# A preparation stage with two inverse roots placed in PSUM, an early root on ScalarE, and one step moved ahead of another on VectorE

## The chip, the cores and the metric

The kernel runs on one core of a Trainium2 chip. The metric is the device time of one execution in microseconds (us). Engines are named as in the profile: PE is TensorE's matmul (PEld its weight load), DVE is VectorE, ACT is ScalarE, POOL is GpSimd, SP is SyncE, which here only issues DMAs. "SPq" or "ACTq" is an engine's sequencer.

## The reference

Two layers over x of 16 batches, 512 tokens and 128 features, all fp32. Each layer adds an attention part and a feed-forward part to its input, both computed from the layer-normed input `xn`.

```python
# layer 0, attention part (16 heads of 8 features)
static_out = xn @ W.T
k = xn_by_head * rsqrt(mean(xn_by_head ** 2) + eps) * k_norm_w     # q = k
for each token:                                                    # gated delta rule
    S = lam * S
    S = S + beta * outer(k, v - k^T S)
    o = q^T S
out = layernorm(static_out + o) * o_norm_w + o_norm_b
# layer 0, feed-forward part: ternary weights 128 -> 512 -> 512 -> 512 -> 128
# layer 1: linear attention with a decay gamma ** position, and one linear map with a low-rank term
```

## The kernel before

The program has two blocks with a barrier between them. `prepare` computes, batch after batch, all that the token recurrence needs: the layer norm of x, the keys, the products of neighbouring keys, and a small triangular solve inside each group of four tokens. It stores the results to DRAM. `recur_and_second_layer` runs the recurrence, the feed-forward part and the second layer. The change lies wholly in `prepare`.

`prepare` is written by hand, engine by engine. Each engine runs its own list of steps in order, and semaphores tie the lists together. A loop counter k runs over the rounds, and one round works on four batches at once, each at another depth: batch k is normed, k-1 gets its keys, k-2 its products, k-3 its solve. DVE's round is:

```python
at(of(k), statistics)
at(of(k), aggregate)
if 0 <= k - 3 < NG - 1:
    lower(k - 3)
at(of(k - 1), square_sums)
at(of(k - 3), solve, 0)
at(of(k), scale)
at(of(k), offset)
at(of(k - 3), solve, 1)
at(of(k - 2), products)
at(of(k - 3), solve, 2)
at(of(k - 1), inverse_rms)
at(of(k - 1), keys)
```

- `scale` (L575) takes the reciprocal of the four standard deviations `std`; `offset` (L579) multiplies minus the mean (`mv`) by it to give `nm`. ACT's `norm` (L450) reads both and writes `xn`.
- `inverse_rms` (L590) takes 64 reciprocals; `keys` (L595) multiplies `xn` by them. PE's `keys` (L722) turns the result into `ps_k`.
- `solve` is `sweep` (L258 and L262), three times with 384, 256 and 128 elements. DVE's copy reads `ps_n` and keeps its product in `tmp_r`, which is a part of the PSUM bank `ps_t`. POOL does the same on SBUF tiles `tmp_p` and `pp`. POOL also scales the keys twice (L362, L370).
- `products` (L606) reads the keys in PSUM and in SBUF. PE's `couplings` (L737) reads the result, and ACT's `couplings` (L489) brings PE's result back for the next solve.
- PE's round is `static` (L729), `couplings` (L737), `keys` (L722), `normed` (L714), `factors` (L747), `weights` (L757). `weights` waits for ACT's `factors` (L496), which reads the bank that `factors` on PE has filled. PE's `factors` waits for DVE's `lower` (L623), which reads the bank that `weights` has filled. `lower` is there in ten of the rounds.

In round k = 1 DVE does two things once: `decays` (L643, L644), which waits for ACT's `exponentials` (L505, L506), and `added_row` (L652 to L657), which waits for the seven small DMAs of L324. POOL's `head_factors` (L415 to L427) waits for `decays`, and `products` waits for `head_factors`. PE starts with the transpose of W (L762) into `ps_t`, which waits for the DMA of W; ACT's `static_weights` (L510) copies it out. ACT loads a table of functions where a step needs another one than the step before.

## Time and profile before

| | us |
|---|---|
| median of 3 runs | 841.22 |
| lowest and highest of the 3 | 840.68, 842.06 |
| the profiled execution, its own time | 839.79 |
| its span in the profile | 838.1 |
| DVE busy in the span | 746.7 (89%) |
| PE busy in the span | 748.6 (89%) |
| POOL busy, ACT busy | 624.0 (74%), 590.5 (70%) |

The profile is of one execution. Its span runs from the first instruction of the program to the end of the last. The view of windows gives the busy time of each engine in a stretch of the span; the view of lines groups instructions by the line of the kernel and by shape; the timeline lists them in order of time, with the idle time before each in square brackets and what ended it; the view of waits sums that idle time by who waited for whom.

### The profile page before, as it was taken

Reading aid. Unit: us, or ns where it says so; the run is one execution under the profiler, and the core shown is the slowest. Engines: PE = TensorE matmul, PEld = TensorE weight load, DVE = VectorE, ACT = ScalarE, POOL = GpSimd, SP = SyncE. Lnnn points to the kernel's source line nnn. Section 1 sums busy time; section 2 is a strip of 40 time slices with the busy share of each in tenths; the row PEclk is TensorE's granted clock in tenths of the full one; section 3 lists DMA queues with packets and bytes.
Section 4 is the critical chain, followed back from the end, with each engine's and each line's share of the span. In section 5 each row is a group of like instructions: output and inputs, shape, how many; then the busy total and the mean of one; then the engine's idle time right before and its main releaser. Section 6 shows DMA issues by size and latency. Waiting matters only on the chain.

```text
span 838.1 us, 12725 instructions
## 1 busy us (share of the span) xinstructions
PE 748.6 (89%) x3427; PEld 533.7 (64%) x3427; DVE 746.7 (89%) x1391; ACT 590.5 (70%) x1349; POOL 624.0 (74%) x608
## 2 busy tenths in 40 slices
PE   3989797578999999999999999998679999999996
PEld 2544343246877877877887878885246666666664
DVE  5899999699999999999999999999868989899886
ACT  6887775577778878777797778777367666666631
POOL 3677879478697677777777767865579989899872
PEclk9899988689999999999999999999699999999999
DMA  5577554700600616115052143060133221312000
GB/s 150 178 256 255 203 195 155 174 22 14 139 24 15 138 38 137 38 38 113 24 108 68 38 89 74 0 174 23 34 110 101 64 89 56 97 51 63 14 27 26
DMA packets 136064, 75.68 MB, mean 90 GB/s; under 512 B 74826, under 2 KB 118860, under 8 KB 136012
## 3 DMA queue, kind: packets, MB, share of 16 engines
q1 hardware_dynamic: 134956, 74.58, 32.2%
q10 hardware_dynamic: 1056, 0.52, 0.2%
q8 instruction: 18, 0.29, 0.2%
q14 instruction: 34, 0.28, 0.1%
HBM read 39.86 MB, written 33.55 MB: 88 GB/s over the span
## 4 chain that ended last, share of the span: by engine, by line
DVE 51%; PE 25%; issue 3%; POOL 1%; DMA 0%; DVEq 0%; ACT 0%; SPq 0%; POOLq 0%
DVE r_rec L1138 12%; DVE r_pg L1132 11%; DVE r_kw L1141 11%; DVE r_gain L1146 11%; PE f_ps L1901 6%; PE f_ps L1902 6%; DVE r_rec L1151 6%; PE f_ps L1883 4%; PE r_rec L1936 2%; PE r_rec L1930 1%; PE r_rec L1920 1%; PE f_ps L1909 1%; DVE l_qs L1186 1%; PE r_rec L1918 1%; PE f_ps L1874 1%
## 5 line engine op out<-in xcount | busy, mean ns | idle before, releaser
L1263 POOL TENSOR_TENSOR f_hl<-f_h,f_hh 128x512 fp32r<-128x512 f32 x64 | 82.4, 1293 | 83.6 <-ACT f_hh L1516 83.5
L1380 POOL TENSOR_TENSOR l_kv<-l_qkv 128x1024 f32<-128x1024 f32 x64 | 125.0, 1952 | 23.7 <-PE f_ps L1902 21.0
L1776 PE MATMUL f_ps<-f_gh,w_hi 128*128 128x512 f32 x256 | 102.7, 401 | 7.6 <-POOL f_gl L1263 7.6
L1138 DVE TENSOR_REDUCE r_rec<-r_pg 128x64 f32<-128x576 f32 x128 | 97.4, 761 | 7.2
L1776 PE MATMUL f_ps<-f_hh,w_hi 128*128 128x512 f32 x256 | 101.3, 396 | 0.4 <-ACT f_b L1505 0.4
L1186 DVE TENSOR_TENSOR l_qs<-f_ps,l_qd 128x1024 f32<-128x1024 f32 x64 | 78.3, 1224 | 23.7 <-PE f_ps L1902 11.4
L1271 POOL TENSOR_TENSOR f_g<-f_a,f_b 128x512 f32<-128x512 f32 x64 | 82.0, 1294 | 16.2 <-ACT f_b L1505 16.2
L1146 DVE TENSOR_REDUCE r_gain<-r_kw 128x128 f32<-128x512 f32 x128 | 87.8, 686 | 4.4
L1263 POOL TENSOR_TENSOR f_gl<-f_g,f_gh 128x512 fp32r<-128x512 f32 x64 | 82.4, 1300 | 2.8 <-ACT f_gh L1511 2.8
L1193 DVE TENSOR_REDUCE l_o_in<-l_qs 128x128 f32<-128x1024 f32 x64 | 77.6, 1212 | 0.7
L1511 ACT ACTIVATE f_gh<-f_g 128x512 fp32r<-128x512 f32 x64 | 41.1, 642 | 52.2 <-POOL f_g L1271 51.7
L1778 PE MATMUL f_ps<-f_gl,w_hi 128*128 128x512 f32 x192 | 76.2, 397 | 0.0
L1778 PE MATMUL f_ps<-f_hl,w_hi 128*128 128x512 f32 x192 | 75.0, 391 | 0.0
L1776 PE MATMUL f_ps<-f_xh,w_hi 128*128 128x512 f32 x128 | 54.1, 423 | 22.9 <-ACT f_a L1501 14.8
L1901 PE MATMUL f_ps<-l_kv,tri 128*128 128x512 f32 x128 | 68.1, 614 | 6.7 <-DVE l_qs L1186 6.1
L1815 PE MATMUL f_ps<-w,f_e 128*128 128x128 f32 x512 | 69.6, 280 | 0.0
L1902 PE MATMUL f_ps<-l_kv,tri 128*128 128x512 f32 x128 | 66.2, 599 | 0.0
L1815 PEld LDWEIGHTS f_ps<-w,f_e 128*128 128x128 f32 x512 | 64.5, 198 | 0.0
L1515 ACT ACTIVATE f_h<-f_ps,t 128x512 f32<-128x512 f32 x64 | 44.7, 698 | 27.6 <-PE f_ps L1783 27.5
L1665 ACT ACTIVATE l_qkv<-f_ps 128x384 f32<-128x384 f32 x64 | 31.3, 489 | 46.4 <-PE f_ps L1883 44.9
L1776 PEld LDWEIGHTS f_ps<-f_gh,w_hi 128*128 128x128 f32 x256 | 49.4, 193 | 20.9 <-POOL f_gl L1263 8.6
L1883 PE MATMUL f_ps<-l_w_second,l_xnT 128*128 128x384 f32 x128 | 53.8, 503 | 2.5 <-ACT l_qkv L1665 0.9
(219 smaller groups left out, 2088.8 us busy)
## 6 DMA issues: line engine op xcount, KB each, us to landing
scratch_xnT<-p_xnT SPq DMA_DIRECT2D x16, 256.0 KB, 2.0
scratch_K<-p_kout SPq DMA_DIRECT2D x16, 256.0 KB, 2.3
scratch_fac<-p_fac SPq DMA_DIRECT2D x16, 256.0 KB, 2.0
scratch_R<-p_rr SPq DMA_DIRECT2D x16, 256.0 KB, 2.8
scratch_P<-p_pp SPq DMA_DIRECT2D x16, 256.0 KB, 2.4
first_x<-scratch_xnT SPq DMA_DIRECT2D x16, 256.0 KB, 2.8
first_xt<-in_L_attn_x_dram SPq DMA_DIRECT2D x16, 256.0 KB, 3.0
scratch_W<-r_w SPq DMA_DIRECT2D x16, 256.0 KB, 4.3
```

Source lines behind the costliest of these rows:

```text
L1132: dve.tensor_tensor(pg[q][:, at, :, :, 0:DH].rearrange("p (v g) i k -> p v g i k", g=G), by_head(state[q]), of_tokens(tok_p[u], t), ALU.mu ...
L1138: dve.tensor_reduce(w, pg[q][:, at, :, :, :], AX.X, ALU.add).then_inc(w_ok, 1)
L1141: dve.tensor_tensor(kw[:, :, :].rearrange("p (v g k) i -> p v g k i", v=DH, g=G), w.rearrange("p (v g) i -> p v g i", g=G).unsqueeze(3).to ...
L1146: dve.tensor_reduce(gain[:, :], kw[:, :, :], AX.X, ALU.add).then_inc(gain_ok, 1)
L1263: pool.tensor_tensor(lower, full, upper.bitcast(F32), ALU.subtract).then_inc(done, 1)
L1380: pool.tensor_tensor(dst, k, v, ALU.mult).then_inc(kv_ok, 1)
L1776: nc.tensor.matmul(bank, c.w_hi[:, weights[k], :], upper[k], start=k == 0, stop=False)
L1778: nc.tensor.matmul(bank, c.w_hi[:, weights[k], :], lower[k], start=False, stop=False)
L1815: ins = nc.tensor.matmul(y_at[:, tokens], e_f[:, k, tokens], c.w3[:, k, :], start=False, stop=t == NT - 1 and k == NB - 1)
L1883: nc.tensor.matmul(ps_q[:, 0:3, :].rearrange("p a b -> p (a b)"), xnT[m % XTS][:, t, :], w_second[:, 0:3 * P], start=True, stop=True).then ...
L1901: nc.tensor.matmul(ps_s[:, 0, :], c.tri[:, :], kv[s % 2][:, 0, :], start=True, stop=True)
L1902: nc.tensor.matmul(ps_s[:, 1, :], c.tri[:, :], kv[s % 2][:, 1, :], start=True, stop=True).then_inc(tri_mm, 1)
```

## The change

It makes five edits in `prepare`:

1. `rrms`, the 64 reciprocals that `keys` reads, is a part of the PSUM bank `ps_t` (columns 384 to 447) and no longer an SBUF tile. `tmp_r` uses columns 0 to 383 of that bank.
2. `scale` computes its four reciprocals twice, first into `rstd_ps` (columns 508 to 511 of `ps_t`), then into the SBUF tile `rstd`. `offset` reads the one in PSUM. ACT's `norm` reads the one in SBUF, as before.
3. ACT takes one square root of a constant before its first round, as soon as the constants are there.
4. In round 1, DVE's `added_row` stands ahead of `decays`.
5. The transpose of W goes to the bank `ps_s` in place of `ps_t`.

```diff
--- before.py
+++ after.py
@@ -154,10 +154,11 @@
         x_in = two("x", tile)
         stats = sb("stats", [P, NT, 6])
         mv = sb("mv", [P, NT, 2])
+        first_root = sb("first_root", [P, 1])
         std, rstd, nm = sb("std", [P, NT]), sb("rstd", [P, NT]), sb("nm", [P, NT])
         xn = two("xn", tile)
         sq = sb("sq", tile)
-        ssq, rms, rrms = sb("ssq", [P, NT * H]), sb("rms", [P, NT * H]), sb("rrms", [P, NT * H])
+        ssq, rms = sb("ssq", [P, NT * H]), sb("rms", [P, NT * H])
         keys_t = sb("keys", tile)
         xnT, kT = two("xnT", [P, L]), two("kT", [P, L])
         k2 = sb("k2", [P, L])
@@ -172,6 +173,8 @@
         ps_t = ctx.enter_context(nc.psum_tensor("p_ps_t", [P, L], F32))
         in_ps = ps_n[:, :, 0:NSEG * (BLK - 1) * BSEG].rearrange("p d (s n) -> p d s n", s=NSEG)
         tmp_r = ps_t[:, 0:(BLK - 1) * NSEG * BSEG].rearrange("p (d s b) -> p d s b", d=BLK - 1, s=NSEG)
+        rrms = ps_t[:, L - P:L - P + NT * H]
+        rstd_ps = ps_t[:, L - NT:L]
 
         x_ready = two_sems("x_ready")
         stat, aggregating, stat_ok, std_ok, rstd_ok, nm_ok = (sem("stat"), sem("aggregating"), sem("stat_ok"), sem("std_ok"),
@@ -507,7 +510,7 @@
 
                 def static_weights():
                     act.wait_ge(ws_tr, 1)
-                    act.activation(c.ws_t[:, :], ps_t[:, 0:P], ACT.Copy).then_inc(ws_ok, 1)
+                    act.activation(c.ws_t[:, :], ps_s[:, 0, :], ACT.Copy).then_inc(ws_ok, 1)
 
                 def lay_first_group():
 
@@ -530,6 +533,7 @@
                 act.sem_inc(coup_ok, 1)
                 act.sem_inc(fac_ok, 1)
                 act.wait_ge(const_done, 1)
+                act.activation(first_root[:, :], c.eps_ln[:, :], ACT.Sqrt)
                 for k in range(B + 3):
                     at(of(k), root)
                     at(of(k - 2), keys)
@@ -572,11 +576,12 @@
 
                 def scale(l):
                     dve.wait_ge(std_ok, l.count(1, 1))
+                    dve.reciprocal(rstd_ps, std[:, :])
                     dve.reciprocal(rstd[:, :], std[:, :]).then_inc(rstd_ok, 1)
 
                 def offset(l):
                     dve.wait_ge(rstd_ok, l.count(1, 1))
-                    dve.scalar_tensor_tensor(out=nm[:, :], in0=mv[:, :, 0], scalar=-1.0, in1=rstd[:, :],
+                    dve.scalar_tensor_tensor(out=nm[:, :], in0=mv[:, :, 0], scalar=-1.0, in1=rstd_ps,
                                              op0=ALU.mult, op1=ALU.mult).then_inc(nm_ok, 1)
 
                 def square_sums(m):
@@ -587,14 +592,14 @@
 
                 def inverse_rms(m):
                     dve.wait_ge(rms_ok, m.count(1, 2))
-                    dve.reciprocal(rrms[:, :], rms[:, :]).then_inc(rrms_ok, 1)
+                    dve.reciprocal(rrms, rms[:, :]).then_inc(rrms_ok, 1)
 
                 def keys(m):
                     dve.wait_ge(k_tr, m.count(1, 1))
                     dve.wait_ge(rrms_ok, m.count(1, 1))
                     dve.tensor_tensor(keys_t[:, :, :].rearrange("p t (h k) -> p (t h) k", h=H),
                                       xn[m.slot][:, :, :].rearrange("p t (h k) -> p (t h) k", h=H),
-                                      rrms[:, :].unsqueeze(2).to_broadcast([P, NT * H, DH]), ALU.mult).then_inc(keys_ok, 1)
+                                      rrms.unsqueeze(2).to_broadcast([P, NT * H, DH]), ALU.mult).then_inc(keys_ok, 1)
 
                 def products(n):
                     dve.wait_ge(n_mm, n.count(1, 1))
@@ -699,8 +704,8 @@
                     at(of(k - 1), inverse_rms)
                     at(of(k - 1), keys)
                     if k == 1:
+                        added_row()
                         decays()
-                        added_row()
                     largest(k)
                 powers()
                 whether_lower()
@@ -759,7 +764,7 @@
 
                 pe.wait_ge(const_done, 4)
                 pe.wait_ge(ws_in, 16)
-                nc.tensor.transpose(ps_t[:, 0:P], nat_ws[:, :], c.ident[:, :]).then_inc(ws_tr, 1)
+                nc.tensor.transpose(ps_s[:, 0, :], nat_ws[:, :], c.ident[:, :]).then_inc(ws_tr, 1)
                 for k in range(1, B + 3):
                     at(of(k - 2), static)
                     if k < B + 2:
```

Where it moves instructions. First DVE, around its one-time steps in round 1 (`p_work` are the decays, `one_rows`, `p_o_hi` and `ob_rows` the added row). Before:

```order
L590 RECIPROCAL p_rrms<-p_rms 128x64
L595 TENSOR_TENSOR p_keys<-p_xn,p_rrms 128x512
L643 TENSOR_SCALAR p_work<-p_work 128x2
L644 RECIPROCAL p_work<-p_work 128x2
L652 CAST one_rows<-p_ones 128x128
L653 CAST p_o_hi<-p_o_bias 64x128
L654 CAST ob_rows<-p_o_hi 32x512
L655 TENSOR_TENSOR ob_rows<-p_o_bias,p_o_hi 32x512
L657 CAST ob_rows<-p_o_bias 64x512
L563 BN_STATS p_stats<-p_x 128x6 x4
```

With the change, whose lines stand up to five further down:

```order
L595 RECIPROCAL p_ps_t<-p_rms 128x64
L600 TENSOR_TENSOR p_keys<-p_xn,p_ps_t 128x512
L657 CAST one_rows<-p_ones 128x128
L658 CAST p_o_hi<-p_o_bias 64x128
L659 CAST ob_rows<-p_o_hi 32x512
L660 TENSOR_TENSOR ob_rows<-p_o_bias,p_o_hi 32x512
L662 CAST ob_rows<-p_o_bias 64x512
L648 TENSOR_SCALAR p_work<-p_work 128x2
L649 RECIPROCAL p_work<-p_work 128x2
L567 BN_STATS p_stats<-p_x 128x6 x4
```

The five instructions of the added row stand ahead of the two of the decays, and the statistics of batch 2 still follow both. Then ACT at its start. Before:

```order
L526 DMA p_x<-in_L_attn_x_dram 128x4x128 x2
L444 ACT_TABLE_LOAD
L444 ACTIVATE p_std<-p_mv,eps_ln 128x4
L450 ACTIVATE p_xn<-p_x,p_nm,p_rstd 128x128 x4
L457 ACTIVATE p_sq<-p_xn 128x512
```

With the change:

```order
L529 DMA p_x<-in_L_attn_x_dram 128x4x128 x2
L536 ACT_TABLE_LOAD
L536 ACTIVATE p_first_root<-eps_ln 128x1
L447 ACTIVATE p_std<-p_mv,eps_ln 128x4
L453 ACTIVATE p_xn<-p_x,p_nm,p_rstd 128x128 x4
```

The load of the root's table stands at an instruction that waits only for POOL's constants, and the root of batch 0 follows without a load. Last, DVE in a middle round. Before:

```order
L262 TENSOR_TENSOR p_rr<-p_rr,p_ps_t 128x3x8x16
L575 RECIPROCAL p_rstd<-p_std 128x4
L579 SCALAR_TENSOR_TENSOR p_nm<-p_mv,p_rstd 128x4
L258 TENSOR_TENSOR p_ps_t<-p_ps_n,p_rr 128x256
L262 TENSOR_TENSOR p_rr<-p_rr,p_ps_t 128x2x8x16
```

With the change:

```order
L265 TENSOR_TENSOR p_rr<-p_rr,p_ps_t 128x3x8x16
L579 RECIPROCAL p_ps_t<-p_std 128x4
L580 RECIPROCAL p_rstd<-p_std 128x4
L584 SCALAR_TENSOR_TENSOR p_nm<-p_mv,p_ps_t 128x4
L261 TENSOR_TENSOR p_ps_t<-p_ps_n,p_rr 128x256
```

One reciprocal of four elements is added, and the instruction behind it has one input in SBUF and one in PSUM where it had two in SBUF.

## Rows read from the trace of the kernel before

**Rows 1.** Windows: stretch, us; busy us of PE, PEld, DVE, ACT, POOL; PE clock, DMA, GB/s.

```profile
27.00:110.00 83.00, 71.36 (x258) 36.52 (x257) 78.68 (x229) 65.91 (x158) 65.45 (x80) 0.92 0.70 232
110.00:155.00 45.00, 35.50 (x107) 16.22 (x105) 40.17 (x94) 29.46 (x67) 38.34 (x46) 0.89 0.45 161
```

**Rows 2.** Lines by shape, DVE, 0 to 160 us: busy us, mean ns, idle before.

```profile
L258 DVE TENSOR_TENSOR p_ps_t<-p_ps_n,p_rr 128x384 f32<-128x384 f32 x16 | 9.0, 560 | 4.3 <-ACT p_coup L489 4.3
L262 DVE TENSOR_TENSOR p_rr<-p_rr,p_ps_t 128x384 f32<-128x384 f32 x16 | 8.9, 554 | 0.5
...
L623 DVE TENSOR_TENSOR w_lo<-p_ps_f,w_hi 128x512 fp32r<-128x512 f32 x10 | 6.6, 658 | 0.0
```

**Rows 3.** One line each: durations in ns as least/median/most.

```profile
L579 DVE SCALAR_TENSOR_TENSOR p_nm<-p_mv,p_rstd x16: 161/600/995, 6.9 to 128.2; 128x4 f32<-128x4 f32 x16
...
L575 DVE RECIPROCAL p_rstd<-p_std x16: 168/170/177, 6.7 to 128.0; 128x4 f32<-128x4 f32 x16
...
L595 DVE TENSOR_TENSOR p_keys<-p_xn,p_rrms x16: 691/946/1575, 11.5 to 138.1; 128x512 f32<-128x512 f32 x16
```

**Rows 4.** Timeline, 69 to 70.4 us: start, us, engine, line, operation.

```profile
69.22 1.03 POOL L370 TENSOR_TENSOR p_kout<-p_kT,kfac 128x512 f32<-128x512 f32 x1
69.27 0.99 DVE L579 SCALAR_TENSOR_TENSOR p_nm<-p_mv,p_rstd 128x4 f32<-128x4 f32 x1
```

**Rows 5.** Timeline, the start of the program, 5 to 21 us.

```profile
5.07 1.28 ACT L444 ACT_TABLE_LOAD   x1 [5.07 <-DVE p_mv L570]
...
8.02 0.45 PE L762 MATMUL p_ps_t<-ident,p_nat_ws 128*128 128x128 f32 x1 [8.02 <-DMA p_nat_ws<-in_L_attn_W_dram]
...
9.14 0.58 SPq L324 DMA_DIRECT2D p_o_bias<-in_L_attn_o_norm_b_dram  x2
...
14.69 0.17 DVE L643 TENSOR_SCALAR p_work<-p_work 128x2 f32<-128x2 f32 x1 [2.51 <-ACT p_work L506]
...
14.97 0.21 DVE L652 CAST one_rows<-p_ones 128x128 fp32r<-128x128 f32 x1
...
16.98 0.87 DVE L563 BATCH_NORM_STATS2 p_stats<-p_x 128x6 f32<-128x128 f32 x4
...
18.40 0.30 ACT L444 ACTIVATE p_std<-p_mv,eps_ln 128x4 f32<-128x4 f32 x1 [2.45 <-DVE p_mv L570]
...
20.35 2.12 PE L729 MATMUL p_ps_s<-p_xnT,ws_t 128*128 128x512 f32 x2 [4.18 <-ACT p_xnT L466]
```

**Rows 6.** DMA issues, 3 to 11 us: KB each, median us from issue to landing.

```profile
p_x<-in_L_attn_x_dram SPq DMA_DIRECT2D x1, 256.0 KB, 3.0
```

**Rows 7.** Timeline of one middle round, PE, with DVE's last sweep and aggregation.

```profile
62.79 1.96 PE L729 MATMUL p_ps_s<-p_xnT,ws_t 128*128 128x512 f32 x2
...
63.79 0.29 DVE L262 TENSOR_TENSOR p_rr<-p_rr,p_ps_t 128x128 f32<-128x128 f32 x1
...
64.57 1.48 PE L737 MATMUL p_ps_n<-p_prod,head_ones 128*128 128x384 f32 x6
...
66.54 0.38 DVE L570 BATCH_NORM_AGGREGATE p_mv<-p_stats 128x2 f32<-128x6 f32 x4 [0.16 <-DVE p_stats L563]
```

**Rows 8.** Waits, 27 to 110 us: who waited for whom, us, times, longest.

```profile
PE p_ps_f L757 <- ACT p_fac L496: 10.3, 10, 1.8
...
PEld p_ps_f L747 <- issue: 2.1, 4, 0.8
```

**Rows 9.** Lines by shape, DVE, 27 to 110 us.

```profile
L595 DVE TENSOR_TENSOR p_keys<-p_xn,p_rrms 128x512 f32<-128x512 f32 x10 | 9.6, 956 | 1.0
...
L579 DVE SCALAR_TENSOR_TENSOR p_nm<-p_mv,p_rstd 128x4 f32<-128x4 f32 x10 | 6.9, 693 | 0.3
```

**Rows 10.** Waits, 110 to 132 us.

```profile
PE p_ps_n L737 <- DVE p_rr L262: 2.4, 3, 1.0
DVE p_ps_t L258 <- ACT p_coup L489: 0.7, 1, 0.7
```

**Rows 11.** Lines by shape, DVE, 110 to 132 us.

```profile
L579 DVE SCALAR_TENSOR_TENSOR p_nm<-p_mv,p_rstd 128x4 f32<-128x4 f32 x3 | 1.8, 598 | 0.1
```

## The prediction

> **What bounds the kernel now.** I began with the windows. The preparation ends at about 155 us, and the change touches nothing behind it. In its long middle, 27 to 110 us, DVE is busy 78.7 of 83 us and PE 71.4; from 110 to 155 us DVE is busy 40.2 of 45 us and PE 35.5 [rows 1]. So DVE is nearly full there, and PE is not far behind.
>
> Next, the lines by shape: does DVE's busy time consist of work? Two of its operations have durations that don't fit their size. `offset` (L579) works on four elements a partition and takes from 161 to 995 ns, while the reciprocal ahead of it on as many elements never takes over 177. `keys` (L595) takes from 691 to 1575 ns at one shape [rows 3]. The timeline shows what it is in one case: POOL starts a scaling of the keys at 69.22 and DVE `offset` at 69.27, and DVE's ends at 70.26, where POOL's ends [rows 4]. Both DVE operations have two inputs in SBUF, as POOL's has. The sweeps, which have one in PSUM, take 560 and 554 ns in the mean [rows 2] and show nothing like it. I read the excess as DVE standing at an SBUF interface that POOL holds.
>
> Third, the waits, for who takes over when DVE gets faster. In one middle round PE runs `static` from 62.79 to 64.75 and starts `couplings` right behind it at 64.57 (a matmul's end is modelled), while DVE's last sweep, for which `couplings` waits, was done at 64.08 [rows 7]. PE was the later one. Only ahead of `factors` (L747), which needs DVE's `lower`, does DVE hold it, and from 27 to 110 us that is 2.1 us in four waits [rows 8]. The 10.3 us in ten waits for ACT's factors [rows 8] are part of PE's own loop, since ACT waits for PE's matmul there. From 110 to 132 us it is the other way round: the weights are done, and PE waits for DVE's last sweep in each of three rounds, 2.4 us in all [rows 10].
>
> **The parts of the change.**
>
> *Inputs in PSUM, on DVE.* From 27 to 110 us there are ten rounds. `offset` falls from 693 ns to the 161 that it takes undisturbed: 10 x 0.53 = 5.3 us. `keys` falls from 956 to 691: 10 x 0.265 = 2.65 us [rows 3, 9]. The added reciprocal has no row at its place. A reciprocal of this size shows 170 ns [rows 3], which is the upper bound; four aggregations in a row take 0.38 us together [rows 7], so that one more small instruction behind another costs under 0.1, and I put the lower bound at 0.05. I take 0.1, because it too stands directly behind one without a wait between: -1.0 us. DVE is relieved by 6.9 us in this stretch.
>
> A PSUM operand could cost more than an SBUF one. The sweep that reads and writes PSUM takes 560 ns, the one that writes SBUF 554, and `lower` with one input in PSUM takes 658 for 512 elements [rows 2], under the 691 of `keys`. So I add nothing. The Trainium skill, in "VectorE: DVE Perf Modes" under "The TRN2 errata", gives VectorE 58 cycles of fixed cost from SBUF and 120 from PSUM at 0.96 GHz, which speaks against this change. By that rule, as an estimate, each of the 32 changed instructions would cost 65 ns more, 2.1 us of DVE in all, and the total below would be 0.2 smaller, since PE hides it in the middle. The rows do not bear it out.
>
> *What of it reaches the end.* In the middle PE takes over: of DVE's 6.9 us only the 2.1 that PE waited for `lower` come through. **2.1 us.** From 110 to 132 us DVE sets the pace in three rounds: `offset` saves 598 - 161 - 100 = 0.34 us each, 1.0 us [rows 3, 11]. `keys` stands ahead of DVE's wait for ACT's couplings, 0.7 us in one of these rounds [rows 10], so its 0.26 counts in one of the others, and perhaps in two. **1.3 us.** Behind 132 us no `offset` is left.
>
> *The root's table.* The load of 1.28 us at 5.07 waits for DVE's first statistics [rows 5]. Ahead of the first round it lies in the wait for x, and costs nothing: ACT has only issued two DMAs by then. The first batch is 1.28 us earlier, but PE waits for W's DMA until 8.02 [rows 5] ahead of its first transposes, so that some 0.3 us of it pass to what follows. The move of W's transpose to `ps_s` is one instruction for one, at the same time, and is costed at nothing; its bank is free until `static`.
>
> *The added row.* DVE idles 2.51 us ahead of the decays at 14.69, and the added row then takes from 14.97 to 16.98, 2.0 us [rows 5]. Put ahead, it fills the idle time. It adds a wait for the seven small DMAs, behind which decays, statistics of batch 2 and all of DVE are queued. The last of them are issued at 9.14 to 9.72 [rows 5]; the next DMA on the queue lands 3.0 us after its issue [rows 6], so I take 12.4 us. The row ends at 14.4, the decays are through at 14.8, and the statistics start there instead of at 16.98: 2.2 us earlier. They release ACT's root at 18.40, ACT's copies behind it release PE's `static` at 20.35, which PE had waited for during 4.2 us [rows 5], so all three engines move by this. POOL's head factors start no later than now. **2.2 us**, of which the table's 0.3 is a part; bounds 0.6 (should DMAs delay the row to 14) and 2.5.
>
> Sum: 2.1 + 1.3 + 2.2 = 5.6 us. The profiled execution takes 839.8 us by its own time, with 838.1 in its span and 1.7 around it, and would take 834.2. The median of the runs is 1.4 above it, so I predict **835.6 us**.
>
> **The rivals.**
>
> *PE does not bind (a chance of 0.12).* PE's loop holds modelled ends and granted clocks of 0.92 and 0.89 [rows 1]; were it to run at full clock more of the time because its own waits shrink, DVE's whole 6.9 us could come through in the middle: 2.2 + 6.9 + 1.3 = 10.4 us, 830.8 us. For it speaks that DVE is fuller than PE; against it, row by row, that PE's `couplings` started at PE's convenience in the middle.
>
> *The PSUM inputs don't help (0.15).* If DVE stood still for another reason, both operations keep their excess, and 16 reciprocals add 0.1 each, hidden in the middle, 0.3 behind it. Left are the head's 0.6 to 2.2 us: 839.3 to 840.9, of which half is within 0.2%. The even durations of the sweeps and of `lower`, which have one input in PSUM and run beside POOL [rows 2], speak against it. [...]
>
> *Partly swallowed (0.09).* The head's gain and the first rounds' are given back at a store or load that is late (DMA is 0.70 busy in the middle [rows 1]): a gain under 1.7 us, 840 us.
>
> *Slower (0.03).* The clock. PE has 0.92 and 0.89 of its clock in the preparation [rows 1], so some 8 of 83 and 5 of 45 us are lost to stretches at 1.2 GHz, half its full rate of 2.4. An earlier end moves all later stages against such stretches. For the whole to be slower by 1.7 us, over 7.3 us must be given back, that is 15 us more at 1.2 GHz than now. I price it at 843 us. Nothing in the rows asks for it.
>
> **How the numbers follow.** A measurement of this kernel can tell about 0.2%, 1.7 us, from no change. The forecast, 3.5 to 8 us gained, has 0.61. Faster: 0.61 + 0.12 + half of 0.15, 0.81 when rounded up; slower 0.03; the rest, 0.16, within 0.2%. The range leaves out the slower case, most of "PE does not bind" and the ends of the others: 832.3 to 839.5 us.
>
> **What would show it.** `offset` at 0.16 to 0.18 us in all 16 rounds and `keys` at 0.66 to 0.70, with little spread; the statistics of batch 2 near 14.8 and `static` of batch 1 near 18.2; from 27 to 110 us, DVE's busy share well below its 0.95, with waits ahead of the sweep for ACT's couplings, and PE without waits for `lower`; the preparation ending near 149.5 instead of 155. I am wrong in the middle if the rounds get shorter by over 0.4 us each, in the mechanism if `offset` still reaches 0.5 us, and in the head if the added row starts behind 13 us.

## The result, and the profile after

| | before | with the change |
|---|---|---|
| median, us | 841.64 | **835.51** |
| lowest and highest, us | 840.65, 844.67 | 830.63, 839.62 |
| executions | 8 | 8 |
| the profiled execution, its own time | 839.79 | 839.62 |
| its span | 838.1 | 837.9 |

The change makes the kernel faster, by a ratio of 0.9917 with a 95% interval of 0.9894 to 0.9940: 6 to 7 us. 835.6 was forecast. But the two profiled executions are almost equally long, since that of before is shorter than any of its eight comparison runs and that of the change is the longest of its eight. So the pair of traces alone would say that the change did nothing, and several things below rest on more than this pair.

The windows of the changed kernel, with the columns of [rows 1]:

```profile
27.00:110.00 83.00, 71.13 (x260) 37.57 (x260) 71.54 (x238) 65.33 (x158) 61.39 (x79) 0.92 0.71 231
110.00:155.00 45.00, 33.10 (x101) 15.42 (x100) 36.44 (x92) 27.92 (x62) 35.25 (x45) 0.83 0.48 171
```

DVE went from 78.7 busy us to 71.5 in the middle, while PE stays at 71.1. DVE has over 11 idle us there, and the clock of PE is no better than before. The three DVE operations that the edits touch, as in [rows 3] (ns, least/median/most):

```profile
L584 DVE SCALAR_TENSOR_TENSOR p_nm<-p_mv,p_ps_t x16: 157/159/160, 5.8 to 125.8; 128x4 f32<-128x4 f32 x16
...
L600 DVE TENSOR_TENSOR p_keys<-p_xn,p_ps_t x16: 687/687/689, 10.8 to 135.6; 128x512 f32<-128x512 f32 x16
...
L579 DVE RECIPROCAL p_ps_t<-p_std x16: 176/178/186, 5.5 to 125.6; 128x4 f32<-128x4 f32 x16
```

`offset` had taken up to 995 ns and `keys` up to 1575. Neither now varies by more than 3 ns. The start of the program, as in [rows 5]:

```profile
2.14 1.28 ACT L536 ACT_TABLE_LOAD   x1 [2.14 <-issue]
...
5.48 0.19 DVE L579 RECIPROCAL p_ps_t<-p_std 128x4 f32<-128x4 f32 x1 [0.36 <-ACT p_std L447]
5.57 0.15 DVE L580 RECIPROCAL p_rstd<-p_std 128x4 f32<-128x4 f32 x1
...
7.96 0.45 PE L767 MATMUL p_ps_s<-ident,p_nat_ws 128*128 128x128 f32 x1 [7.96 <-DMA p_nat_ws<-in_L_attn_W_dram]
...
12.47 0.23 DVE L657 CAST one_rows<-p_ones 128x128 fp32r<-128x128 f32 x1 [0.95 <-DMA p_o_bias<-in_L_attn_o_norm_b_dram]
...
14.43 0.17 DVE L648 TENSOR_SCALAR p_work<-p_work 128x2 f32<-128x2 f32 x1
...
14.71 0.85 DVE L567 BATCH_NORM_STATS2 p_stats<-p_x 128x6 f32<-128x128 f32 x4
...
18.07 2.12 PE L734 MATMUL p_ps_s<-p_xnT,ws_t 128*128 128x512 f32 x2 [3.38 <-ACT p_xnT L469]
```

The added row starts at 12.47 and the decays end behind it at 14.8. The statistics of batch 2 come at 14.71 in place of 16.98, and `static` of batch 1 at 18.07 in place of 20.35: 2.3 us earlier. The two reciprocals start 0.09 us apart.

Then the middle. PE's `factors` starts once a round, so the distance of its starts is the length of a round. The timeline of PE, from 47 us:

```profile
47.48 1.88 PE L752 MATMUL p_ps_f<-p_k,head_ones 128*128 128x512 f32 x2
...
58.95 1.87 PE L752 MATMUL p_ps_f<-p_k,head_ones 128*128 128x512 f32 x2
...
66.63 1.88 PE L752 MATMUL p_ps_f<-p_k,head_ones 128*128 128x512 f32 x2
...
74.32 1.88 PE L752 MATMUL p_ps_f<-p_k,head_ones 128*128 128x512 f32 x2
...
82.01 1.88 PE L752 MATMUL p_ps_f<-p_k,head_ones 128*128 128x512 f32 x2
```

One round takes 11.47 us and the next three 7.68, 7.69 and 7.69. Taken so, the first thirteen rounds of some executions are:

| | rounds, us | first ten |
|---|---|---|
| before | 7.63 8.08 8.36 8.61 8.06 8.65 7.75 9.40 8.41 8.53, 9.06 7.24 7.42 | 83.5 |
| change | 7.63 7.63 7.68 **11.47** 7.68 7.69 7.69 **11.25** 7.69 7.69, 6.75 **9.20** 6.75 | 84.1 |

The rounds of before vary. Those of the change are alike (7.63 to 7.69 us in the first ten, 6.75 behind them), except for three. Inside the first long one, the timeline of all engines:

```profile
50.44 0.60 ACT L482 ACTIVATE p_rr<-p_ps_s 128x512 f32<-128x512 f32 x1 [1.84 <-DMA scratch_R<-p_rr]
...
51.17 0.68 ACT L499 ACTIVATE p_fac<-p_ps_f,gate 128x512 f32<-128x512 f32 x1
...
51.99 1.08 PE L762 MATMUL p_ps_f<-ident,p_nath 128*128 128x128 f32 x4 [2.64 <-ACT p_fac L499]
...
54.68 2.74 PE L742 MATMUL p_ps_n<-p_prod,head_ones 128*128 128x384 f32 x6
...
57.52 0.93 ACT L492 ACTIVATE p_coup<-p_ps_n 128x384 f32<-128x384 f32 x3 [2.61 <-PE p_ps_n L742]
...
58.48 0.57 DVE L261 TENSOR_TENSOR p_ps_t<-p_ps_n,p_rr 128x384 f32<-128x384 f32 x1 [3.30 <-ACT p_coup L492]
```

Read it from the top. ACT's copy of `static` into `rr` (L482) waits 1.84 us for the store that still reads this buffer; `rr` has two. `factors` on ACT is queued behind it. PE's `weights` waits for that 2.64 us, where it waits 0.92 in an undisturbed round. And then the same six matmuls of `couplings` take 2.74 us, where they take 1.48 [rows 7]. The windows around it give the reason:

```profile
42.00:49.00 7.00, 6.41 (x26) 3.41 (x26) 6.64 (x24) 5.69 (x14) 5.15 (x7) 1.00 1.00 342
49.00:52.00 3.00, 0.36 (x2) 0.04 (x1) 2.83 (x9) 1.56 (x4) 2.88 (x4) 0.87 0.58 205
52.00:59.00 7.00, 7.00 (x25) 5.04 (x26) 3.54 (x12) 4.15 (x12) 2.88 (x5) 0.57 0.67 214
59.00:66.00 7.00, 6.08 (x23) 2.73 (x22) 6.60 (x24) 5.96 (x14) 5.82 (x8) 1.00 0.54 174
```

PE works 0.36 of 3 us from 49 to 52, and from 52 to 59 its granted clock is 0.57 in the mean, most of the time at 1.2 GHz in place of 2.4. PE is busy for all 7.00 us, and DVE and ACT wait for it. So a store for which ACT waits 1.8 us costs 11.47 - 7.69 = 3.8 us. The waits say how often this happened, from 27 to 110 us and then from 110 to 132:

```profile
PE p_ps_f L762 <- ACT p_fac L499: 12.5, 10, 2.6
...
DVE p_ps_t L261 <- ACT p_coup L492: 7.4, 4, 3.3
...
ACT p_rr L482 <- DMA scratch_R<-p_rr: 3.6, 2, 1.8
```

```profile
ACT p_rr L482 <- DMA scratch_R<-p_rr: 2.0, 1, 2.0
```

Two long rounds and then one: three waits, three long rounds.

An undisturbed round has PE's steps at fixed distances: `weights` 2.79 us behind `factors`, `couplings` 2.24 behind that, `keys` 1.31, `normed` 0.89, and the next `factors` 0.44. Ten such rounds make 76.8 us (two at 7.64, as the first two are, and eight at 7.69). What an execution takes more can be split: what `factors` comes later than 0.44 us behind `normed` is its wait for DVE's `lower`; the rest is everything else: late stores and the waits behind them, stretches at half clock, and `couplings` or `keys` that start later because DVE's results come later.

| first ten rounds, us | sum | above 76.8 | wait for `lower` | rest |
|---|---|---|---|---|
| before | 83.5 | 6.7 | 2.0 | 4.7 |
| change | 84.1 | 7.3 | 0.0 | 7.3 |

PE no longer waits for `lower`, the 2.1 us of [rows 8] are gone, and the rest is larger in this execution. (That row names "issue" and not `lower`; but in each of those rounds `lower` ends 0.10 us before `factors` starts.) Whether the change makes it larger is a question for the experiments.

### The profile page after: what moved, and what is told of

It reads as the page before. It is cut to its first block, busy times and chain, and to the rows that moved or that the text cites. A ratio compares the mean times of both kernels' runs of the same rounds, so it can differ in the third digit from the quotient of the medians.

```text
span 837.9 us, 12741 instructions
## 1 busy us (share of the span) xinstructions
PE 747.6 (89%) x3427; PEld 534.2 (64%) x3427; DVE 740.3 (88%) x1407; ACT 591.0 (71%) x1350; POOL 619.2 (74%) x608
## 4 chain that ended last, share of the span: by engine, by line
DVE 51%; PE 25%; issue 3%; POOL 1%; DMA 1%; ACT 0%; DVEq 0%; SPq 0%; POOLq 0%
DVE r_rec L1143 12%; DVE r_pg L1137 11%; DVE r_kw L1146 11%; DVE r_gain L1151 11%; PE f_ps L1906 6%; PE f_ps L1907 6%; DVE r_rec L1156 5%; PE f_ps L1888 4%; PE r_rec L1941 2%; PE r_rec L1935 1%; PE r_rec L1925 1%; PE f_ps L1914 1%; DVE l_qs L1191 1%; PE r_rec L1923 1%; PE f_ps L1879 1%
## 5 line engine op out<-in xcount | busy, mean ns | idle before, releaser
L1268 POOL TENSOR_TENSOR f_hl<-f_h,f_hh 128x512 fp32r<-128x512 f32 x64 | 82.6, 1296 | 83.1 <-ACT f_hh L1521 83.0
L1781 PE MATMUL f_ps<-f_xh,w_hi 128*128 128x512 f32 x128 | 54.1, 423 | 22.4 <-ACT f_a L1506 14.8
```

Source lines behind the costliest of these rows:

```text
L1268: pool.tensor_tensor(lower, full, upper.bitcast(F32), ALU.subtract).then_inc(done, 1)
L1781: nc.tensor.matmul(bank, c.w_hi[:, weights[k], :], upper[k], start=k == 0, stop=False)
```

## The experiments

Twelve runs follow, two of them repeats of the kernels themselves, each beside the kernel before on the same chip. "Preparation ends" is the start of the second block's first load in the profiled execution.

| | median, us (lowest to highest, runs) | before | ratio, 95% | preparation ends |
|---|---|---|---|---|
| before, first trace | | | | 158.97 |
| change | 835.51 (830.63 to 839.62, 8) | 841.64 | 0.9917 (0.9894 to 0.9940) | 156.78 |
| e1, change again | 834.80 (833.17 to 838.95, 6) | 841.71 | 0.9918 (0.9900 to 0.9936) | 155.70 |
| e2, head only | 839.31 (836.82 to 840.86, 11) | 841.71 | 0.9962 (0.9948 to 0.9976) | 159.09 |
| e3, PSUM only | 838.67 (838.08 to 838.90, 5) | 841.71 | 0.9961 (0.9946 to 0.9976) | 157.44 |
| e4, twins in SBUF | 839.56 (837.59 to 843.25, 12) | 841.71 | 0.9978 (0.9965 to 0.9992) | 157.49 |
| e5, third `rr` | **829.60** (827.59 to 831.49, 5) | 842.33 | **0.9840** (0.9819 to 0.9861) | 149.03 |
| e6, less on DVE | 837.66 (835.64 to 838.36, 4) | 842.33 | 0.9934 (0.9910 to 0.9959) | 155.39 |
| e7, two roots | 836.29 (834.69 to 837.73, 4) | 842.33 | 0.9927 (0.9902 to 0.9953) | 155.11 |
| e8, row only | 839.54 (837.63 to 842.48, 10) | 842.33 | 0.9967 (0.9953 to 0.9980) | 158.40 |
| e9, before again | 842.51 (839.81 to 844.27, 10) | 841.47 | 1.0003 (0.9984 to 1.0023) | 161.79 |
| e10, before, third `rr` | 838.30 (836.21 to 841.51, 10) | 841.47 | 0.9964 (0.9943 to 0.9985) | 156.77 |
| e11, third `rr` and `pp` | 830.11 (826.74 to 832.92, 6) | 841.47 | 0.9854 (0.9826 to 0.9883) | 148.50 |
| e12, offset only | 837.39 (834.89 to 838.77, 10) | 841.47 | 0.9944 (0.9927 to 0.9961) | 153.70 |

### Is the trace of the change an odd one? (e1)

The changed kernel without an edit, for a second profile.

> The changed kernel as it is, for a second profile and more times. Theory: the time of an execution hangs on how many rounds of the preparation are long (over 9 us where the others take 7.7), because a store of rr lands late, ACT's copy waits, PE stands idle and its clock falls to 1.2 GHz. Then this profile has another number of such rounds than the three of the first profile (839.6 us), each worth some 2 to 4 us, and the times spread over 830 to 840 us with a median near 835.5. Rival: the spread arises in the second block; then the preparation ends at the same 156.8 us in both profiles, and the difference of the spans lies behind it.

The second profile has the same three long rounds, of 11.74, 10.65 and 8.91 us, and 7.64 to 7.69 in the others of the first ten. ACT waits for the stores of `rr` 5.7 us in all (6.4 in the first profile). So the long rounds belong to this kernel and not to one execution. This profiled execution was again the longest of its kernel, 838.95 us; its preparation is 1.1 us shorter than the first's, and the second block 0.4 us longer. Why the profiled executions of the change are long was not found.

### The parts alone (e2, e3, e8)

e2 has the root's table and the added row, with the inputs in SBUF as before (edits 3 and 4). e3 has the inputs in PSUM and W's transpose (edits 1, 2 and 5), and e8 the added row alone (edit 4). The edits, in part:

```diff
 # e2, against the change; W's transpose goes to ps_t again
-        rrms = ps_t[:, L - P:L - P + NT * H]
-        rstd_ps = ps_t[:, L - NT:L]
-                    dve.reciprocal(rstd_ps, std[:, :])
 # e3, against the change
-                act.activation(first_root[:, :], c.eps_ln[:, :], ACT.Sqrt)
-                        added_row()
                         decays()
+                        added_row()
 # e8, against before
+                        added_row()
                         decays()
-                        added_row()
```

> Only the early root and the added row ahead of the decays (edits 3 and 4). Theory: PE's static of batch 1 starts at 18.1 us instead of 20.35, and the preparation ends 2.2 us earlier: a median of 839.3 (before 841.5). Offset keeps its 160 to 995 ns and keys its 690 to 1575. Rival (the head's gain is given back in the middle by the late DMAs): static at 18.1, but 841 us.

> Only the inputs in PSUM (edits 1, 2 and 5). Theory: offset at 0.16 us and keys at 0.69 in all rounds, undisturbed rounds of 7.7 us instead of 8.1 to 8.6, and a gain of 3.4 us, 838 us, with a spread of several us. Rival (PE alone binds and the DVE relief is worth nothing): under 1 us gained, 840.7 or more.

> Only the added row ahead of the decays (edit 4), with the table loaded where it was. Prediction's terms: the row starts when the small DMAs are in, near 12.4 us or when keys of batch 0 is done at 12.2, the decays wait for ACT's exponentials until 14.7, so the statistics of batch 2 start at 15.0 instead of 16.98, and PE's static of batch 1 at 18.4: 1.9 of the head's 2.2 to 2.3 us, a median of 839.7. Rival (the early table is what counts): static at 19 us or later.

The head is worth 2.4 us (841.71 to 839.31), and the PSUM inputs 3.0 (to 838.67). Together that is 5.4, and the whole change made 6.1 and 6.9 in its two comparisons, so that the parts add up within what the intervals leave. In e2 `offset` still takes up to 1.08 us and `keys` up to 1.18; in e3 they take 0.16 and 0.69 in all 16 rounds, and `static` of batch 1 starts at 20.37, as before. Of the head, the row alone is worth 2.8 us in its own comparison. Its timeline:

```profile
12.16 0.23 DVE L652 CAST one_rows<-p_ones 128x128 fp32r<-128x128 f32 x1
...
14.57 0.17 DVE L643 TENSOR_SCALAR p_work<-p_work 128x2 f32<-128x2 f32 x1 [0.47 <-ACT p_work L506]
...
14.85 0.85 DVE L563 BATCH_NORM_STATS2 p_stats<-p_x 128x6 f32<-128x128 f32 x4
...
18.20 1.11 PE L729 MATMUL p_ps_s<-p_xnT,ws_t 128*128 128x512 f32 x1 [2.15 <-ACT p_xnT L466]
```

`static` starts at 18.20 without the early table, against 18.07 and 18.11 with it. So the table is worth 0.1 us there and not the 0.3 of the prediction. The reason stands in the second row: the row ends before 14.1, and what remains is a wait of 0.47 us for ACT's exponentials. The table moves only that wait. The row itself starts at 12.16 here, right behind `keys`, but waits for its DMAs until 12.47 and 12.53 in the two traces with the table. With a row as early as here the table would be worth up to 0.45 us, as an estimate (14.57 less the 14.12 at which the row would let the decays start).

### Is it the port? (e4, e12)

e4 keeps every instruction of the change, also the second reciprocal, but puts both results into SBUF. e12 puts only that of `keys` back.

```diff
 # e4
-        rrms = ps_t[:, L - P:L - P + NT * H]
-        rstd_ps = ps_t[:, L - NT:L]
+        rrms = sb("rrms", [P, NT * H])[:, :]
+        rstd_ps = sb("rstd_two", [P, NT])[:, :]
 # e12
-        rrms = ps_t[:, L - P:L - P + NT * H]
+        rrms = sb("rrms", [P, NT * H])[:, :]
```

> The whole change, but rrms and the second copy of the four reciprocals lie in SBUF tiles, so that offset and keys have two inputs in SBUF again. Theory (POOL holds an interface that the second SBUF input needs): offset again takes up to 1 us and keys up to 1.6, rounds are 8.1 to 8.6 us, and only the head's 2.2 us are left, less 0.1 us a round for the added reciprocal: 839.5 to 840.5. Rival (what helps is the second instruction or the separate tile, not the place): offset at 0.16 to 0.2, 835.5.

> The change without edit 1: rrms back in SBUF, so that keys has two inputs in SBUF, while offset keeps one in PSUM. Theory: keys at 0.69 to 1.6 us again, offset at 0.16; undisturbed rounds of 7.7 to 8.1 us, about 1 us of the gain lost: 836 to 837 us. Rival (keys alone matters, since it stands ahead of ACT's couplings): 838.5 us or more.

Two lines in e4:

```profile
L584 DVE SCALAR_TENSOR_TENSOR p_nm<-p_mv,p_rstd_two x16: 161/670/935, 5.6 to 126.8; 128x4 f32<-128x4 f32 x16
...
L600 DVE TENSOR_TENSOR p_keys<-p_xn,p_rrms x16: 692/930/1433, 10.8 to 136.6; 128x512 f32<-128x512 f32 x16
```

and in e12:

```profile
L584 DVE SCALAR_TENSOR_TENSOR p_nm<-p_mv,p_ps_t x16: 157/159/160, 5.8 to 122.9; 128x4 f32<-128x4 f32 x16
...
L600 DVE TENSOR_TENSOR p_keys<-p_xn,p_rrms x16: 691/692/1592, 11.0 to 132.7; 128x512 f32<-128x512 f32 x16
```

The place of one operand decides, operation by operation, and nothing else in the change does. That it is POOL that DVE stands for, no run without POOL's work shows; the traces show it by coincidence in time. In the trace of before, each of the 13 `offset`s that take 320 ns or more ends 0.02 us behind the end of an instruction of POOL, and the three that take under 170 meet none. In the changed kernel 12 of the 16 run wholly inside an instruction of POOL and take no longer for it:

```profile
67.65 1.00 POOL L265 TENSOR_TENSOR p_pp<-p_pp,p_tmp_p 128x384 f32<-128x384 f32 x1
...
67.88 0.16 DVE L584 SCALAR_TENSOR_TENSOR p_nm<-p_mv,p_ps_t 128x4 f32<-128x4 f32 x1
```

e4 ends where e2 and e8 do (839.56 against 839.31 and 839.54), which leaves the whole gain of the middle to that place. In e12 `keys` is undisturbed in most rounds though it has two inputs in SBUF: with `offset` at a constant length, DVE mostly starts `keys` in a gap of POOL or just ahead of its next instruction. In the second case it is POOL that takes longer: its scaling that starts at 61.64, 0.02 us behind `keys`, takes 1.58 us where 1.04 is usual. Even so, e12 at 0.9944 is behind the whole change at 0.9917. The Trainium skill, in "SBUF — State Buffer" under "Who interferes with whom", gives VectorE and GpSimd one shared pair of ports with an exclusive lock; e4 and e12 agree with it, up to 0.9 us for one `keys` (1592 against 691 ns).

### Who binds the short rounds? (e6, e7)

e6 takes work away from DVE: from batch 3 on it leaves out the statistics and their aggregation for all but the first 128 of 512 tokens. e7 adds work: a second reciprocal of 64 elements whose result nobody reads.

```diff
 # e6
-                    for t in range(NT):
+                    for t in range(NT if l.off < 3 else 1):
 # e7, ahead of the reciprocal into rrms
+                    dve.reciprocal(idle_root[m.slot][:, :], rms[:, :])
```

> The whole change, with the statistics of batches 3 to 15 taken over the first 128 of their 512 tokens alone, the other three quarters being those of earlier batches: some 0.8 us less on DVE in each round. It tells whether DVE or PE sets the undisturbed rounds of 7.7 us. Theory of the prediction (PE's own loop binds): these rounds stay at 7.6 to 7.7 us, and the time within 1.5 us of 835. Rival (DVE is still full and binds too, both at 7.69): rounds of 6.9 to 7.3 us and 828 to 831 us.

> The whole change, with the 64 reciprocals of each batch computed once more into a tile that nothing reads: 0.48 to 0.55 us more on DVE in each round, where nothing but DVE does it. If DVE had room behind PE, undisturbed rounds stay at 7.7 us. If DVE is as full as PE there, as its 0.16 us of idle time in such a round says, they grow to 8.2 us, and the time rises by 3 to 5 us to 838 to 840 us.

The middle of e6, as a window and as two successive first sweeps of DVE:

```profile
27.00:110.00 83.00, 71.79 (x261) 37.17 (x261) 65.13 (x180) 65.39 (x159) 62.27 (x80) 0.92 0.71 231
```

```profile
66.04 0.56 DVE L261 TENSOR_TENSOR p_ps_t<-p_ps_n,p_rr 128x384 f32<-128x384 f32 x1 [0.70 <-ACT p_coup L492]
...
73.82 0.56 DVE L261 TENSOR_TENSOR p_ps_t<-p_ps_n,p_rr 128x384 f32<-128x384 f32 x1 [0.80 <-ACT p_coup L492]
```

DVE has 6.4 us less to do than in the change, and six of the ten rounds take 7.63 to 7.69 us as before, none less. In the two shown DVE waits 0.7 and 0.8 us. (The other four are 11.42, 7.78, 8.77 and 9.74 us; ACT waits for stores of `rr` around them.) So DVE does not set a round of 7.69. What is left is PE's loop, with the 0.92 us in which it waits for ACT's factors, and the change has brought DVE just below it.

e7 shows the other side. The extra reciprocal costs DVE some 0.5 us a round, and four of the ten rounds are 7.96 to 8.09 us, where PE again waits for `lower` (1.4 us in all). I had expected 838 to 840 us; it took 836.29, a ratio of 0.9927 against the change's 0.9917. The expectation was missed because the long rounds are shorter, 9.84 and 10.27 us in place of 11.47 and 11.25, at a granted clock of 0.83 in place of 0.70. In the first of them the store is less late (ACT waits 1.12 us, 1.84 in the change), in the second it is not (1.75 against 1.79), and why that one is shorter too was not found. One more round takes 8.53 us at a clock of 0.80, without a late store. Its first ten rounds sum to 83.8 us, those of the change to 84.1. So what DVE takes or gives in the other rounds was offset in the long ones, and the time hardly moved.

### The late stores (e5, e10, e11)

e5 is the change with three tiles for `rr` and a semaphore for each; to free one, the load of gamma is counted together with two others, in e11 also the last weight with `lower`. e10 is the kernel before with the same edit. e11 is e5 with three tiles for `pp` too. The edits, in part:

```diff
 # e5 and e10; e11 has the same for pp and st_p
-        rr, pp = two("rr", [P, L]), two("pp", [P, L])
+        rr, pp = [sb(f"rr{u}", [P, L]) for u in range(3)], two("pp", [P, L])
+        st_r = [sem(f"st_r{u}") for u in range(3)]
...
-                    reuse(act, st_r[m.slot], both(m))
+                    reuse(act, st_r[m.off % 3], 32 * (m.off // 3))
```

> The whole change, and a third tile for rr, the solved values that are stored to DRAM, so that ACT's copy of batch n waits for the store of batch n-3 and no longer of n-2 (one semaphore less elsewhere: gamma's DMA is counted with first_in). Theory (late stores of rr make ACT wait, then PE idles and loses half its clock): no wait of ACT's copy for scratch_R, no round over 8.5 us, twelve rounds of 7.7 us and less, the preparation ends some 6 to 9 us earlier in the profile, and the median falls from 835 to 829 to 832. Rival (the long rounds come from the clock or from DMA load as such): long rounds stay at 9 us or more, within 1 us of 835.

> The kernel before with the third tile for rr alone. Theory (DVE sets its rounds of 8.1 to 8.6 us, the late stores add little there): rounds of 8.0 to 8.3 us without long ones, and 2 to 4 us gained, 838 to 840 us; the third tile is worth 5 to 6 us only where DVE has been relieved. Rival (the two add up and have nothing to do with each other): 6 us gained, 836 us or less.

> The change with the third tile for rr and one more for pp, which POOL's scaling waits for (POOL waited 7.9 us in all for stores of pp in the run with the third rr; PE's w3 signal is counted with lo_done to free a semaphore). Theory (POOL is not on the loop that sets the rounds, but ACT's couplings wait for its solve once or twice): 0 to 2 us better than 829.6 us. Rival (POOL's lateness passes to SP's stores and from there to x): 3 us or more better.

The windows of e5, and its PE at the place of the long round (its lines stand two further down than those of the change):

```profile
27.00:110.00 83.00, 73.91 (x282) 37.03 (x283) 77.94 (x261) 71.98 (x174) 67.83 (x87) 1.00 0.76 249
```

```profile
47.75 1.88 PE L754 MATMUL p_ps_f<-p_k,head_ones 128*128 128x512 f32 x2
50.54 0.63 PE L764 MATMUL p_ps_f<-ident,p_nath 128*128 128x128 f32 x4 [0.92 <-ACT p_fac L501]
...
52.79 1.48 PE L744 MATMUL p_ps_n<-p_prod,head_ones 128*128 128x384 f32 x6
...
55.43 1.88 PE L754 MATMUL p_ps_f<-p_k,head_ones 128*128 128x512 f32 x2
```

The round takes 7.68 us. The first ten are all between 7.63 and 7.69, 76.8 us in all, against 84.1 for the change: nothing is left above the undisturbed rounds. PE has its full clock through the whole middle, `weights` waits 0.92 us and never more, and ACT has no wait for a store of `rr` in the whole preparation. It ends at 149.03, 7.8 us before that of the change. **829.6 us, 1.6% under the kernel before**: this version beats both kernels.

e10 separates the two: the third tile alone is worth 3.2 us on the kernel before (841.47 to 838.30). On the changed kernel it is worth 5.8 to 6.6 (the 12.7 of e5 less the 6.1 or 6.9 of the change). The split of the rounds says why. In e10 `offset` still reaches 0.99 us and `keys` 1.24; the rest is down to 2.3 us, but PE waits 3.9 us for `lower`. With no late stores the rounds fall back on DVE, unless DVE too has been relieved.

The 2.3 us are DVE's too, though ACT waits for no store of `rr` in e10. The windows from 27 to 110 us and of its round from 58.59, and the waits of PE's weight loads for DVE's products from 27 to 110 us in e10 and in e5:

```profile
27.00:110.00 83.00, 71.16 (x261) 34.71 (x260) 78.66 (x230) 67.32 (x161) 66.60 (x81) 0.98 0.71 234
58.59:67.12 8.53, 7.61 (x27) 4.15 (x27) 8.13 (x24) 6.49 (x17) 6.80 (x9) 0.80 0.80 253
```

```profile
PEld p_ps_n L739 <- DVE p_prod L608: 13.2, 10, 1.8
```

```profile
PEld p_ps_n L744 <- DVE p_prod L613: 3.4, 3, 2.1
```

(Most of the weight loads' waits lie beside running matmuls and cost nothing.) This round takes 8.53 us at a clock of 0.80, with no late store and no idle time of PE over 0.92 us. e5 differs from e10 by the edits of the change alone, and its ten rounds take 76.8 us in place of 83.1. So with the late stores out of the way, the inputs in PSUM are worth 6.3 us in the ten rounds, close to the 6.9 that DVE was to be relieved by.

e11 gives nothing beyond e5 (0.9854 against 0.9840): POOL's waits for stores of `pp`, 7.9 us in e5, are not on the path.

### Was the first trace of before an odd one? (e9)

The kernel before without an edit.

> The kernel before as it is, for a second profile. Its first profile (839.8 us) was among the fastest of its executions, those of the change among the slowest. Theory (the first profile of before had few late stores): this one has a preparation that ends at 160 to 162 us instead of 158.97, with longer waits of ACT's copy for scratch_R than 2.6 us in all. Rival: it ends at 159 within 0.5 us, and what profiles of the change show as lost in the middle is lost in unprofiled executions too.

The waits of ACT and POOL for stores up to 162 us:

```profile
POOL p_pp L362 <- DMA scratch_P<-p_pp: 5.6, 4, 3.0
ACT p_rr L479 <- DMA scratch_R<-p_rr: 4.1, 3, 2.4
```

Its preparation ends at 161.79, 2.8 us behind that of the first trace. Its rounds are 8.07 8.58 8.15 **11.63** 7.68 8.45 8.45 9.55 8.02 8.84, 87.4 us for the ten. The kernel before has the long round too, and ACT waits 4.1 us for the stores of `rr` where it was 2.6 in the first trace. Against this trace the change gains 3.3 us in the ten rounds (87.4 to 84.1); against the first it loses 0.6.

All traces together, split as above:

| first ten rounds, us | inputs | sum | wait for `lower` | rest |
|---|---|---|---|---|
| before | SBUF | 83.5 | 2.0 | 4.7 |
| e9, before again | SBUF | 87.4 | 3.4 | 7.3 |
| e2, head only | SBUF | 86.4 | 2.0 | 7.6 |
| e8, row only | SBUF | 85.7 | 2.6 | 6.3 |
| e4, twins in SBUF | SBUF | 85.3 | 3.8 | 4.8 |
| e10, third `rr` | SBUF | 83.1 | 3.9 | 2.3 |
| change | PSUM | 84.1 | 0.0 | 7.3 |
| e1, change again | PSUM | 83.8 | 0.0 | 7.0 |
| e3, PSUM only | PSUM | 83.4 | 0.0 | 6.6 |
| e7, two roots | PSUM | 83.8 | 1.4 | 5.6 |
| e6, less on DVE | PSUM | 83.7 | 0.0 | 6.9 |
| e12, offset only | `offset` alone | 82.7 | 0.4 | 5.5 |
| e5, third `rr` | PSUM | 76.8 | 0.0 | 0.0 |
| e11, third `rr` and `pp` | PSUM | 76.8 | 0.0 | 0.0 |

The wait for `lower` is 2.0 to 3.8 us with the inputs in SBUF and two tiles for `rr`, and none with both in PSUM. The rest is 4.7 to 7.6 us (6.1 in the mean of five) with the inputs in SBUF and 6.6 to 7.3 with them in PSUM (7.0 in the mean of the change, e1 and e3). But it is not the same rest. With the inputs in SBUF 2.3 us of it stay when no store is late (e10), with them in PSUM nothing does (e5).

The sums put it together. Two tiles for `rr`: 85.7 us in the mean of five with the inputs in SBUF, 83.8 in the mean of three with them in PSUM, 1.9 us gained. Three tiles: 83.1 and 76.8, 6.3 us gained. Or read the other way, late stores cost 2.6 us in the ten rounds before and 7.0 with the change. So 4.4 of the 6.3 us that the inputs in PSUM bring are taken back at late stores. The traces with three tiles are one or two of a kind, and single traces of before differ by 3.9 us, but the medians say the same: with three tiles the inputs in PSUM are worth 5.8 to 7.2 us (e11 and e5 against e10, less 2.4 for the head), with two 3.0 to 4.5 (e3 against before, e1 against e2).

## Why the prediction was right, and where it was not

**The port: right.** `offset` was to take 0.16 to 0.18 us and `keys` 0.66 to 0.70, with little spread. They take 0.157 to 0.160 and 0.687 to 0.689 in all 16 rounds, and e4 and e12 show that the operand's place is the cause.

**The price of a PSUM operand: nothing, as taken.** `keys` takes 687 ns with one input in PSUM and 691 undisturbed with two in SBUF; `offset` takes 159 against 161. The Trainium skill, in "VectorE: DVE Perf Modes" under "The TRN2 errata", has 120 cycles of fixed cost from PSUM and 58 from SBUF at 0.96 GHz, as an estimate 65 ns more for each; that is not borne out here.

**The added reciprocal: 0.09 us, 0.1 was taken.** Also right is its argument, that a small instruction directly behind another costs less than the duration in its row, 178 ns.

**The head: 2.2 us forecast, 2.3 measured** at `static` of batch 1 and 2.4 in the median of e2. The start of the row (12.4 forecast, 12.47), the statistics (14.8, 14.71) and `static` (18.2, 18.07) all came where they were put. Inside it the table was over-sized: 0.1 and not 0.3.

**110 to 132 us: the size was right, 1.3 us forecast.** The three rounds take 22.7 us, before 23.7; in the means of three traces with the inputs in PSUM and five with them in SBUF it is 22.6 and 23.8, 1.2 us less. Two of the three take 6.75 us, where before had 7.24 and 7.42: 0.5 and 0.7 us less, more than the 0.34 of `offset` with `keys` in one or two. The third takes 9.20 because of a late store (before: 9.06, with no late store and a clock of 0.81).

**The middle: the size came out, the account of it only in part.** "In the middle PE takes over: of DVE's 6.9 us only the 2.1 that PE waited for `lower` come through." Right is that the wait, 2.0 us in the ten rounds of that trace, is 0.0 now, and that PE's loop sets the undisturbed round (e6). In the medians the PSUM inputs are worth 3.0 us alone (e3) and 4.5 on top of the head in the same comparison (839.31 in e2, 834.80 in e1), against the 3.4 of this term and the last together. Wrong is "Only ahead of `factors` (L747) [...] does DVE hold it", which was read off one round [rows 7]: with the late stores out of the way 6.3 us come through and not 2.1 (e10 to e5). DVE's lateness costs PE also ahead of `couplings` and `keys`, and in its clock. In the trace of before the window of one such round, with no late store, shows it:

```profile
67.60:76.24 8.64, 7.72 (x26) 4.05 (x27) 8.24 (x24) 6.42 (x17) 5.97 (x9) 0.80 0.72 229
```

The second term that the prediction lacks is the late stores, which take 4.4 of the 6.3 us back. Neither amount is in the sum, they nearly offset each other, and that about 2 us are left is luck.

**The sum: 5.6 forecast, 6.1 and 6.9 measured.** The forecast of 835.6 against 835.51 is closer than the parts allow one to claim, the middle above all.

**What failed is what the two profiles would show.** The preparation was to end "near 149.5 instead of 155". 155 is only where the window of [rows 1] ends; in the trace of before the second block starts at 158.97. The end was to come 5.6 us earlier, and comes 2.2 us earlier in the first pair of traces (158.97 to 156.78), but 5.0 to 6.1 against e9 (161.79 to 156.78 and 155.70). The sum was made against the profiled execution, with 1.4 us added for the median: that trace was not only short by 1.4 us as a whole, it was short by some 3 in this very stage, where waits for stores differ from one execution to the next.

The sign "I am wrong in the middle if the rounds get shorter by over 0.4 us each" came true, and rightly. The undisturbed rounds are 0.66 us below the mean of before (8.35 to 7.69), since more of DVE's relief comes through in them than the prediction let through. The mean of all ten does not show it, because two long rounds stand among them.

**What was not seen: the rest.** The forecast asked for the next limit behind DVE and found PE's loop, but read the clock of 0.92 [rows 1] as given. In fact 2.6 us of the middle before, and 7.0 with the change, hung on one cause, a store that still held one of two tiles. The row that says so was in the trace of before, ACT's 2.6 us of waits for the stores of `rr` up to 162 us, in three waits. It looked small because its price is paid elsewhere: in the changed kernel 1.84 us at ACT, 2.64 at PE, 3.8 in the round. (The clock's 0.92 was also priced a little high in the rival "Slower": 0.08 of 83 us are 6.6 and not "some 8".)

**The rivals.** "PE does not bind" is out for this change as it stands: PE binds at 7.69 us. But its arithmetic, DVE's whole 6.9 us through the middle with PE at full clock, is nearly what the third tile lets happen (6.3 us, a clock of 1.00), and its time of 830.8 is about that of e5. "The PSUM inputs don't help" is out by e3 and e4. "Partly swallowed" named a late store, and its mechanism is there: late stores take back 4.4 us in the ten rounds. What it had wrong is from what, since it let the head's gain be eaten and left the middle at 2.1. "Slower" did not come; its mechanism, the clock, is what doubles the price of a late store.

**What stays open.** Why the stores of `rr` are late just at those two or three places was not settled. In the changed kernel they are the stores of batches 2, 6 and 10, issued at 45.80, 80.83 and 114.01; they land 4.6, 4.1 and 4.5 us later, the others 2.3 to 3.6. ACT needs the tile 3.3 us after the issue in an undisturbed round, so there is little room. The DMA share in the window ahead of the first is 1.00, with 342 GB/s, and transfers of weights for the second block are issued there (L339, among the stores). They can't be what delays the third, since the last of them is issued at 89.67; whether they delay the first two was not tried. The second block takes 678.9 to 682.7 us over the fourteen profiles without an edit to its work, and this scatter of nearly 4 us is as large as several effects here. e6 should not be slower than the change, and is in its median of four runs, 837.66 against 835.51 and 834.80, though the intervals of the ratios overlap; that was not explained.

## What to carry to other kernels

Look at the least, the median and the most of one instruction's duration before believing a busy share: where they are far apart on a VectorE operation with two SBUF inputs, put the smaller input in PSUM. Once the fullest engine is relieved, look for the next limit among the buffers too (which store must have read a tile before it is written again), and count with the clock behind each idle gap of PE; the two remedies here brought 3.0 and 3.2 us alone, 8.6 with the 2.4 of the head, and all together 12.7. A remedy that measures small may be one whose gain another limit takes back. And split a loop's rounds into their steps against the shortest round in the trace, and take two profiled executions of each kernel where the effect is under 1%.

## What was not expected of the hardware

- A four-element operation can take six times its undisturbed length (161 against 995 ns) while GpSimd holds SBUF, and a PSUM operand frees it wholly.
- A store that was late by 1.84 us cost 3.8 us, since PE's idle time of 2.64 us was followed by 7 us at a granted clock of 0.57 in the mean.
- The clock fell without a late store too: in the round from 67.60 us of the kernel before, where PE's longest idle time was 0.92 us, the granted clock was 0.80 and the round 8.65 us long.
- With some 0.5 us a round added on DVE the long rounds fell from 11.47 and 11.25 to 9.84 and 10.27 us (e7).
- From 143 us on, where PE has little to do, its clock is low in any case: 0.62 in the change, 0.50 in e5. Part of what e5 gains in the middle may be given back there, but its end still came first.
